# A transformer layer on one core: the end by sequence, feed-forward halves between small products, and three transfers moved

## The chip, the core and the metric

The kernel runs on one core of a Trainium2 chip. TensorE (PE in the profile) multiplies, VectorE (DVE), ScalarE (ACT) and GpSimd (POOL) work on elements, SyncE (SP) issues most transfers. The metric is the device time of one execution in microseconds. The kernel before took 1822.03 us in the median of three runs (1814.67 to 1822.35).

## The reference

The program is one decoder layer on x of 32 sequences, 256 positions, 256 features, in float32:

```python
x = x + attn(layernorm(x))            # causal self-attention, 16 heads of 16, 4 key heads, low-rank q (64) and kv (32), rotary
x = x + xattn(layernorm(x), ctx)      # cross-attention on ctx, 16 heads, masked by an int mask of 256 x 256
x = x + ffn(layernorm(x))             # relu(x @ w1.T + b1) rounded to 8 bits, times w2 rounded to 8 bits, plus b2
```

Softmax is exact: the maximum of each row of scores is subtracted before the exponential. Query and key are each cut into three bf16 parts, stacked to 96 rows (`TERMS = 6` pairs of 16), so that one bf16 product gives a float32 score.

## The kernel before

Two sequences form a group; there are 16 groups. The order of every engine is written by hand, each engine in its own block, tied by semaphores. Three parts make a program: a prologue, `body(i, prev, nxt)` for each group (groups 1 to 14 in a hardware loop), and an end. `prev` means that a group before still has its cross-attention and feed-forward to do, `nxt` that a next group is prepared.

A body on PE goes through these stages:

1. **Cross exponentials** of the group before (`attend(st, 1, i - 1, "scores")`): 16 tiles of transposed scores (`cross_shifted`, L1279), ACT's exponential (L691), DVE's bound for three tiles of four (L922), and the products with the values three tiles later (`times_v`, L1318). The stacked queries carry three more rows, the negated row maxima (`negT`), which come by a transfer (`put_neg`, L372). PE waits for those of the first sequence at tile 0, for the second at tile 8.
2. **Self maxima** (`self_scores`, L1202 and L1213): 12 tiles, each reduced by DVE (L900). PE also does `v2`, `k2_1` and the output product of the group before (L1404).
3. **Self exponentials** (`attend(st, 0, i, None)`, L1256 and L1261): 12 tiles; PE waits for the negated maxima of the second sequence at its seventh tile.
4. **The middle chain**: output product, two normalisations, `query2` (L1165) for each sequence, the small products of the next group, `query1` (`q0`, `q1`, L1173, 64 rows), `key1` (`k`, L1179, 32 rows) and `value1` (`v_0`, `v_1`, L1189, 32 rows), and feed-forward tiles 0 to 2 of the group before (`hidden`, L1149). It takes turns through four PSUM banks (`body_users` says which name stands in which).
5. **Cross maxima** (`cross_scores`, L1237): 16 tiles; ACT lays the mask down (`premask`, L737), DVE reduces (L900), PE does feed-forward tiles 3 to 7 (L1435) and the second feed-forward product (L1451) between them. POOL meanwhile rotates, cuts and rounds the next group's q and k (L509 to L537).

SP issues the transfers that stack the parts: `put_part` (`Q<-q1p`, `K<-k1p`, `K<-k2p`), `put_query2` (`Q<-q2p`), `put_neg`, and `swap_pairs` for the rotation. It waits for each in the order written, so one that isn't ready holds those behind it. POOL ends a body with `add_ffn` (L498), which adds the feed-forward to `x3`, and stores it (L500). DVE waits for the store before last in the next body (`y_stored`) ahead of `residual(st, "out2", 0, ...)`.

In the prologue SP loads x, then 15 weights in one list counted by one semaphore (`loaded`). DVE rotates q, rounds `w2` and only then cuts q; POOL rotates and cuts k (L509 to L537); SP stacks all parts of both (L354, L356); PE waits for all of them before its first score (L1202). The end does both sequences' output product, one normalisation over four blocks, eight feed-forward tiles of 512 columns (L1149), and two output products (L1451).

## Time and profile before

| | us |
|---|---|
| median of three runs | 1822.03 |
| profiled execution | 1819.02 |
| its span, first to last instruction | 1817.0 |
| PE busy | 1673.7 |
| DVE busy | 1245.2 |
| ACT busy | 1103.6 |
| POOL busy | 724.2 |

The span runs from the first instruction to the last; the profiled execution's own time is 2.0 us longer. A busy PE is one that has a matmul under way. The page also shows the clock that PE was granted, as a share of 2.4 GHz. What decides is which wait ends last in a stage, so the stages are read one by one in the rows further down.

### The profile page before, as it was taken

What the parts mean: (1) busy time and instruction counts of PE and PEld (TensorE: products, weight loads), DVE (VectorE), ACT (ScalarE), POOL (GpSimd) and SP (SyncE); (2) the same over time, 40 slices, a digit from 0 to 9 for tenths busy, and PEclk for the clock granted to TensorE, in tenths of its full rate; (3) what the DMA queues carried; (4) which work ended last, traced back from release to release, by engine and by line L of the source; (5) the groups of instructions that cost most, each with busy time, mean ns of one, the idle gap of its engine ahead of it and who ended that gap; (6) DMA issues with size and microseconds to landing.
All of it is one profiled execution on the core that took longest, in us unless ns stands there. A gap on an engine that the chain in (4) does not pass through costs nothing.

```text
span 1817.0 us, 34264 instructions
## 1 busy us (share of the span) xinstructions
PE 1673.7 (92%) x12274; PEld 1015.8 (56%) x12274; DVE 1245.2 (69%) x1908; ACT 1103.6 (61%) x1704; POOL 724.2 (40%) x962
## 2 busy tenths in 40 slices
PE   3779999999999999999999999999999999999987
PEld 1445556556555565555556555665655556555554
DVE  4567486785848768586776848678585876858582
ACT  3355675756667565665756567575666756566572
POOL 3251353624435352433634345362443535243310
PEclk9979999999999999999999999999999999999998
DMA  6452552715346251633724255271534625163320
GB/s 170 59 83 39 76 88 36 122 28 85 57 64 100 36 95 38 92 67 43 121 36 79 49 75 88 36 119 30 84 59 62 101 36 95 37 93 57 48 37 12
DMA packets 86606, 124.07 MB, mean 68 GB/s; under 512 B 10481, under 2 KB 53938, under 8 KB 86322
## 3 DMA queue, kind: packets, MB, share of 16 engines
q1 hardware_dynamic: 83650, 115.26, 41.5%
q0 software_dynamic: 2160, 7.87, 1.2%
q10 hardware_dynamic: 768, 0.57, 0.1%
q8 instruction: 18, 0.29, 0.1%
q14 instruction: 10, 0.08, 0.0%
HBM read 21.42 MB, written 8.39 MB: 16 GB/s over the span
## 4 chain that ended last, share of the span: by engine, by line
PE 68%; DVE 10%; issue 7%; ACT 5%; POOL 4%; DMA 3%; SPq 2%; ACTq 0%; POOLq 0%
PE o_pair L1318 12%; PE small L1404 8%; PE small L1149 7%; DVE negmax L900 6%; PE score L1279 6%; PE o_pair L1149 3%; PE small L1331 3%; PE small L1165 3%; PE score L1256 3%; DMA Q<-negT 2%; PE small L1435 2%; PE score L1202 2%; DVE P L922 2%; PE score L1261 2%; ACT P L691 2%
## 5 line engine op out<-in xcount | busy, mean ns | idle before, releaser
L691 ACT ACTIVATE P<-score 128x1024 f32<-128x1024 f32 x448 | 446.8, 1026 | 119.7 <-PE score L1279 42.7
L900 DVE TENSOR_REDUCE negmax<-score 128x4 f32<-128x1024 f32 (+1 forms) x384 | 460.0, 1219 | 32.6 <-PE score L1237 19.8
L922 DVE TENSOR_TENSOR P<-P,cross_bound 128x1024 f32<-128x1024 f32 x192 | 255.6, 1365 | 65.8 <-ACT P L691 65.6
L1318 PE MATMUL o_pair<-P,V 128*32 128x256 f32 (+1 forms) x4096 | 283.1, 363 | 15.6 <-DVE P L922 15.6
L737 ACT ACTIVATE score<-cross_q 128x1024 f32<-128x1024 bf16 x192 | 196.5, 1023 | 60.3 <-DVE negmax L900 58.7
L468 POOL TENSOR_TENSOR negrest<-negmax,negparts 128x32 f32<-128x32 f32 x64 | 15.5, 243 | 502.1 <-ACT negparts L652 501.6
L1318 PEld LDWEIGHTS o_pair<-P,V 128*32 128x32 f32 x4096 | 86.2, 108 | 148.2 <-issue 78.1
L1279 PE MATMUL score<-Q,K 99*128 99x256 bf16 x1024 | 151.5, 275 | 13.3 <-DMA Q<-negT 12.2
L1435 PE MATMUL small<-xnT,w 128*128 128x256 f32 x600 | 156.7, 379 | 0.0
L1237 PE MATMUL score<-K,Q 96*128 96x256 bf16 x768 | 119.5, 279 | 33.8 <-ACT score L737 30.8
L1279 PEld LDWEIGHTS score<-Q,K 99*128 99x128 bf16 x1024 | 85.8, 98 | 100.8 <-issue 66.1
L547 POOL TENSOR_SCALAR_AFFINE_SELECT P<-P 128x512 f32<-128x512 f32 (+1 forms) x160 | 121.1, 757 | 0.0
L461 POOL TENSOR_TENSOR rstd<-vareps,minus_half 128x2 f32<-128x2 f32 x32 | 22.4, 701 | 236.2 <-DVE vareps L881 236.2
L910 DVE RECIPROCAL rsum<-small 128x16 f32<-128x16 f32 x127 | 32.2, 253 | 118.7 <-PE small L1331 118.7
L966 DVE SCALAR_TENSOR_TENSOR q2f<-small,bq,q2p 128x256 f32<-128x256 f32 x64 | 28.0, 479 | 124.3 <-ACT q2p L722 124.3
L1237 PEld LDWEIGHTS score<-K,Q 96*128 96x128 bf16 x768 | 70.6, 99 | 73.3 <-ACT score L737 53.0
L1435 PEld LDWEIGHTS small<-xnT,w 128*128 128x128 f32 x600 | 102.8, 189 | 13.4
L684 ACT ACTIVATE o_sb<-o_pair 128x512 f32<-128x512 f32 x128 | 75.9, 593 | 52.3 <-PE o_pair L1318 52.3
L652 ACT ACTIVATE negparts<-negmax 128x32 bf16<-128x32 f32 x64 | 14.4, 225 | 130.4 <-DVE negmax L900 130.4
L1202 PE MATMUL score<-K,Q 96*128 96x256 bf16 x512 | 78.7, 276 | 6.4 <-DMA Q<-q1p 6.4
L900 DVE TENSOR_REDUCE negmax<-o_pair 128x4 f32<-128x1024 f32 x64 | 78.1, 1221 | 8.2 <-PE o_pair L1242 8.2
L1331 PE MATMUL small<-ident,o_sb 128*128 128x128 f32 x508 | 81.6, 283 | 0.2 <-ACT o_sb L684 0.2
(181 smaller groups left out, 3219.4 us busy)
## 6 DMA issues: line engine op xcount, KB each, us to landing
Q<-q1p SPq DMA_DIRECT2D x96, 256.0 KB, 5.9
K<-k2p SPq DMA_DIRECT2D x96, 256.0 KB, 8.4
Q<-q2p SPq DMA_DIRECT2D x192, 128.0 KB, 4.0
x_in<-in_x SPq DMA_DIRECT2D x16, 512.0 KB, 5.6
ctxT<-in_ctx SPq DMA_DIRECT2D x16, 512.0 KB, 4.4
k2f<-q1f SPq DMA_DIRECT2D x32, 256.0 KB, 5.3
out_y<-x POOLq DMA_DIRECT2D x15, 512.0 KB, 3.6
K<-k1p SPq DMA_DIRECT2D x96, 64.0 KB, 4.5
```

The lines of the kernel that those rows point to most:

```text
L547: G.affine_select(out=p, in_=p, compare_op=ALU.is_ge, fill=0.0, base=0, pattern=[[0, heads], [1, 128]], channel_multiplier=-1).then_inc(pr ...
L691: A.activation(P[:, t % 4, :], score[b][:, :, :], ACT.Exp, scale=SCALE).then_inc(score_free[b], 1)
L737: A.activation(cross_bufs[n][:, :, :].rearrange("p c (j k) -> p (c j) k", j=2), cross_q[:, t // 4 % 2, :].unsqueeze(1).broadcast_to([128, ...
L900: V.tensor_reduce(negmax[:, k, h:h + 1024 // w], s.rearrange("p (h w) -> p h w", w=w), AX.X, ALU.max, negate=True).then_inc(score_free[b], 1)
L922: V.tensor_tensor(p, p, cross_bound[:, t % 2, :].unsqueeze(1).broadcast_to([128, 4, SEQ]), ALU.min).then_inc(probs_masked[1], 1)
L1149: last = T.matmul(bank[0:rows, :], w[:, c, cols], src[:, c, :], start=c == 0, stop=c == NC - 1)
L1237: last = T.matmul(cross_bufs[n][:, c, SEQ * j:SEQ * j + SEQ], Q2[0:KROWS, b, h, 128 * (k % 2):128 * (k % 2) + 128], K2[0:KROWS, h, SEQ * b ...
L1279: last = T.matmul(score[n][:, c, SEQ * j:SEQ * j + SEQ], K2[:, h, SEQ * b + 128 * kb:SEQ * b + 128 * kb + 128], Q2[:, b, h, :], start=j == ...
L1318: last = T.matmul(o_ps[ob][32 * j:32 * j + 32, SEQ * gg + q0:SEQ * gg + SEQ], v, p, start=s == 0, stop=end, tile_position=(0, 32 * j), ski ...
L1331: last = T.transpose(bank[:, 256 * k + 128 * gg:256 * k + 128 * gg + 128], o_sb[:, u % 2, SEQ * gg + 128 * k:SEQ * gg + 128 * k + 128], id ...
L1404: last = T.matmul(bank[:, DM * k:DM * k + DM], src[:, c, at:at + 128], w[:, c, :], start=c == 0, stop=c == NC - 1)
L1435: last = T.matmul(bank[:, half], w1[:, c, 128 * t:128 * t + 128], xnT3[:, c, half], start=p == 0, stop=c == NC - 1, skip_group_check=True)
```

## The change

- **Middle chain.** PE's order becomes `q0`, first half (128 input features) of feed-forward tile 1, `q1`, its second half, `k`, tile 2 in two halves, `xnT2_1`, `v_0`, `v_1`, `query2` of the second sequence. ACT's copies follow the same order, and the banks are dealt anew.
- **Feed-forward addition.** POOL waits, where a next group is prepared, until DVE has reduced tile 0 of the next self maxima, and then does `add_ffn`.
- **Order of transfers.** In a body five of the six `K<-k2p` transfers are issued before the second sequence's `negT` for self-attention. The first sequence's `negT` for cross-attention is issued before `K<-k1p`.
- **Prologue.** mask, b2 and w2 are loaded first with semaphores of their own, and DVE does its mask and rounding work before the rotation. DVE rotates and cuts q of the first sequence, k, and then q of the second. The q parts are stacked by sequence in transfers of 128 KB, the k parts from POOL's queue, and PE begins with what the first sequence needs. ACT's rows of ones are written in pieces.
- **End.** Output product, normalisation, feed-forward and the second product go one sequence after the other, in tiles of 256 columns.

The core of the diff:

```diff
-              + n("qa") + ["xnT2_0", "out1_1", "q2_0"] + n("q0", "q1") + n("k", "v_0", "v_1")
-              + p("h1") + ["xnT2_1"] + p("h2") + ["q2_1"])
+              + n("qa") + ["xnT2_0", "out1_1", "q2_0"] + n("q0") + p("h1") + n("q1", "k") + p("h2")
+              + ["xnT2_1"] + n("v_0", "v_1") + ["q2_1"])
...
+            sp.dma_start(mask[:, :, :], d["mask"]).then_inc(loaded_mask, 16)
+            sp.dma_start(b2[:, :], d["b2"]).then_inc(loaded_w2, 16)
+            sp.dma_start(w2[:, :, :], d["w2"]).then_inc(loaded_w2, 16)
...
-                put_part("k1", n, 0)
-                put_part("q1", n, 0)
+                sp.wait_ge(first_q1, (4, 6, 7)[n])
+                put_queries(n, 0, stacked_first)
+            for n in range(3):
+                sp.wait_ge((part1, part2, part3)[n]["q1"], 1)
+                put_queries(n, 1, stacked["q1"])
...
-                for b in range(GB):
-                    put_neg(st, 0, b)
-                for n in range(3):
+                put_neg(st, 0, 0)
+                for n in range(2):
                     put_part("k2", n, i)
+                put_neg(st, 0, 1)
+                put_part("k2", 2, i)
...
                     put_part("q1", 0, i + 1)
+                put_neg(st, 1, 0)
+                if nxt:
                     put_part("k1", 0, i + 1)
-                put_neg(st, 1, 0)
-                if nxt:
...
-            rope_products("k1", cosk, sink, k1s, 0)
-            rope_sum("k1", k1s, 0)
-            rest("k1", 0)
-            third("k1", 0)
+            for n in range(3):
+                pool.wait_ge((part1, part2, part3)[n]["k1"], 1)
+                for t, p in enumerate(K_PART):
+                    if p == n:
+                        pool.dma_start(K1[HD * t:HD * t + HD], k1p[:, n, :]).then_inc(stacked_first_k1, 16)
...
                 if prev:
+                    if nxt:
+                        n, before = tile("S1", i + 1, 0)
+                        pool.wait_ge(score_free[n], before + 1)
                     add_ffn(st, i - 1)
...
                 if nxt:
                     turn(st, "q1", q1f[:, 1, :])
+                premask(i, 0)
+                if prev:
+                    hidden(st, [1])
+                if nxt:
                     turn(st, "k", k1f[:, :], rows=KV_HEADS * HD)
+                if prev:
+                    hidden(st, [2])
+                turn_batch(st, "xnT2_1", 1, inT)
+                if nxt:
                     values1(st)
-                premask(i, 0)
-                if prev:
-                    hidden(st, [1])
-                turn_batch(st, "xnT2_1", 1, inT)
                 premask(i, 1)
-                if prev:
-                    hidden(st, [2])
                 query2_first(st, i, 1)
                 query2_second(st, 1)
...
+            for b in range(GB):
+                at = range(2 * b, 2 * b + 2)
+                residual(END, "out2", b, x3, x2)
+                residual_done(END, "out2", b)
+                norm_stats(2, x3, NG - 1 + b, at, at)
+                if b == 0:
+                    normalise(END, 1, 3, NG - 1)
+                norm_apply(2, x3, NG - 1 + b, at)
...
-                    for c in range(NC):
-                        query1(st, c)
+                    query1(st, 0)
+                if prev:
+                    hidden_half(st, 1, 0)
+                if nxt:
+                    query1(st, 1)
+                if prev:
+                    hidden_half(st, 1, 1)
+                if nxt:
                     key1(st)
+                if prev:
+                    hidden_half(st, 2, 0)
+                    hidden_half(st, 2, 1)
...
+            batch_copied(END, "oT2_0")
+            tokens(END, "out2", inT, wo2, 0)
+            unit_turn(END, 1, NG - 1, 3)
+            for u in range(2, UNITS):
+                pe.wait_ge(small_free[END.bank(f"o2t{u}")], END.this(f"o2t{u}"))
+            turned_batch(END, "oT2_1", 1, o)
+            pe.wait_ge(xn_ready[2], NG)
+            turned_batch(END, "xnT3_0", 0, xn)
+            batch_copied(END, "oT2_1")
             tokens(END, "out2", inT, wo2, 1)
-            pe.wait_ge(xn_ready[2], NG)
-            for c in range(NC):
-                turned(END, f"xnT3_{c}", xn, c)
-            copied(END, "xnT3_")
-            hidden(END, range(HT))
-            pe.wait_ge(small_free[END.bank(f"h{HT - 1}")], END.this(f"h{HT - 1}"))
-            for r in range(2):
-                ffn_out(END, r)
+            batch_copied(END, "xnT3_0")
+            end_hidden(0)
+            pe.wait_ge(xn_ready[2], NG + 1)
+            turned_batch(END, "xnT3_1", 1, xn)
+            ffn_ready(0)
+            ffn_out(END, 0)
+            batch_copied(END, "xnT3_1")
+            end_hidden(1)
+            ffn_ready(1)
+            ffn_out(END, 1)
```

PE in the loop's middle chain, from `query2` of the first sequence (L1165) to that of the second; `xnT,w` is a feed-forward product, `ident,xn` a transposition. Before:

```order
L1165 MATMUL small<-inT,wq 128x256 x4
L1173 MATMUL small<-qaT,wqb 128x512
L1173 MATMUL o_pair<-qaT,wqb 128x512
L1179 MATMUL o_pair<-qaT,wk 64x512
L1184 REGISTER_ALU
L1189 MATMUL small<-wv,qaT 128x64 x4
L1147 REGISTER_ALU
L1149 MATMUL o_pair<-xnT,w 128x512 x2
L1342 MATMUL o_pair<-ident,xn 128x128 x4
L1147 REGISTER_ALU
L1149 MATMUL small<-xnT,w 128x512 x2
L1358 REGISTER_ALU
L1165 MATMUL small<-inT,wq 128x256 x4
```

After (`query2` is L1239):

```order
L1239 MATMUL small<-inT,wq 128x256 x4
L1247 MATMUL small<-qaT,wqb 128x512
L1223 MATMUL o_pair<-xnT,w 128x512
L1247 MATMUL o_pair<-qaT,wqb 128x512
L1223 MATMUL o_pair<-xnT,w 128x512
L1251 REGISTER_ALU
L1253 MATMUL small<-qaT,wk 64x512
L1223 MATMUL small<-xnT,w 128x512 x2
L1412 REGISTER_ALU
L1416 MATMUL o_pair<-ident,xn 128x128 x4
L1263 MATMUL o_pair<-wv,qaT 128x64 x2
L1258 REGISTER_ALU
L1263 MATMUL small<-wv,qaT 128x64 x2
L1432 REGISTER_ALU
L1239 MATMUL small<-inT,wq 128x256 x4
```

Each feed-forward product of 512 columns now has a small one before or behind it, and the value products stand alone behind the transposition.

SP in the loop from the load of `ctxT` to the loop's end, before:

```order
L412 DMA ctxT<-in_ctx 128x1024
L348 REGISTER_ALU
L356 DMA Q<-q1p 16x8x1024 x3
L354 DMA K<-k1p 16x4x512 x3
L370 REGISTER_ALU
L372 DMA Q<-negT 3x16x256
L356 DMA Q<-q1p 16x8x1024 x2
L354 DMA K<-k1p 16x4x512 x2
L356 DMA Q<-q1p 16x8x1024
L354 DMA K<-k1p 16x4x512
```

After:

```order
L430 DMA ctxT<-in_ctx 128x1024
L351 REGISTER_ALU
L359 DMA Q<-q1p 16x8x1024 x3
L381 REGISTER_ALU
L383 DMA Q<-negT 3x16x256
L357 DMA K<-k1p 16x4x512 x3
L359 DMA Q<-q1p 16x8x1024 x2
L357 DMA K<-k1p 16x4x512 x2
L359 DMA Q<-q1p 16x8x1024
L357 DMA K<-k1p 16x4x512
```

`Q<-negT` went ahead of the three `K<-k1p`.

SP at the loop's self maxima and exponentials, before:

```order
L372 DMA Q<-negT 3x16x256
L370 REGISTER_ALU
L372 DMA Q<-negT 3x16x256
L370 REGISTER_ALU
L372 DMA Q<-negT 3x16x256
L348 REGISTER_ALU
L356 DMA K<-k2p 16x8x1024 x6
```

After:

```order
L383 DMA Q<-negT 3x16x256
L381 REGISTER_ALU
L383 DMA Q<-negT 3x16x256
L351 REGISTER_ALU
L359 DMA K<-k2p 16x8x1024 x5
L381 REGISTER_ALU
L383 DMA Q<-negT 3x16x256
L359 DMA K<-k2p 16x8x1024
```

The third `Q<-negT` is the second sequence's; five transfers of the key stack now stand ahead of it.

## Rows read from the trace of the kernel before

**Rows 1.** Stages; columns: stretch, its us, busy us (instructions) per engine, granted clock, DMA, GB/s.

```profile
868.90:893.90 25.00, 22.09 (x145) 16.26 (x143) 21.30 (x19) 18.62 (x31) 20.80 (x20) 1.00 0.71 113
893.90:915.20 21.30, 20.37 (x191) 9.84 (x191) 17.65 (x20) 16.90 (x21) 6.25 (x5) 1.00 0.48 83
120.40:144.30 23.90, 17.55 (x64) 8.46 (x65) 18.20 (x16) 13.87 (x18) 18.70 (x21) 0.50 0.80 109
1786.00:1796.40 10.40, 7.12 (x14) 3.76 (x15) 1.38 (x4) 1.97 (x4) 1.03 (x1) 0.51 0.00 0
```

**Rows 2.** The same view: ten us from `q0` on, first and last of eight.

```profile
426.70:436.70 10.00, 10.00 (x30) 4.83 (x29) 2.90 (x8) 7.02 (x15) 3.56 (x5) 0.83 0.81 131
...
1614.00:1624.00 10.00, 10.00 (x29) 5.00 (x29) 2.95 (x8) 7.09 (x15) 3.56 (x5) 0.83 0.80 131
```

**Rows 3.** Timeline of PE, middle of two groups; columns: start, us, instruction, [idle before <-releaser].

```profile
430.60 3.45 PE L1149 MATMUL o_pair<-xnT,w 128*128 128x512 f32 x4
...
859.29 1.12 PE L1173 MATMUL small<-qaT,wqb 64*128 64x512 f32 x2
...
863.23 1.98 PE L1149 MATMUL o_pair<-xnT,w 128*128 128x512 f32 x4
...
867.21 1.89 PE L1165 MATMUL small<-inT,wq 128*128 128x256 f32 x8
```

**Rows 4.** Waits of PE over the span: us in total, times, longest.

```profile
PE o_pair L1318 <- DVE P L922: 15.6, 17, 1.3
...
PE score L1279 <- DMA Q<-negT: 12.2, 15, 3.1
```

**Rows 5.** Chain of waits, end of a group; columns: start, us, what.

```profile
890.53 3.24 DMA Q<-negT
...
893.91 1.04 PE score L1279 x8
...
898.35 2.85 DVE P L922
```

**Rows 6.** Timeline of PE, the same place in a group after a half-clock stretch.

```profile
463.10 1.04 PE L1279 MATMUL score<-Q,K 99*128 99x256 bf16 x8 [0.46 <-DMA Q<-negT]
```

**Rows 7.** Timeline, DVE and POOL side by side, and POOL's next wait.

```profile
875.71 2.34 DVE L900 TENSOR_REDUCE negmax<-score 128x4 f32<-128x1024 f32 x2
...
875.81 2.35 POOL L515 TENSOR_TENSOR q1f<-q1f,k2f 128x1024 f32<-128x1024 f32 x1
...
896.99 3.12 POOL L498 TENSOR_TENSOR x<-x,ffn 128x1024 f32<-128x1024 f32 x1
...
925.59 0.24 POOL L468 TENSOR_TENSOR negrest<-negmax,negparts 128x32 f32<-128x32 f32 x1 [23.95 <-ACT negparts L652]
```

**Rows 8.** Timeline of SP's queue: maxima rows and the key stack.

```profile
929.40 10.66 SPq L372 DMA_DIRECT2D Q<-negT  x2
940.18 3.86 SPq L356 DMA_DIRECT2D K<-k2p  x6
```

**Rows 9.** Transfers `K<-k2p` of one group: issue to landing.

```profile
DMA to landing us min/median/max: 4.4/8.3/11.8
```

**Rows 10.** Timeline of PE: seventh tile of the self exponentials.

```profile
943.19 0.60 PE L1256 MATMUL score<-Q,K 99*128 99x512 bf16 x2
```

**Rows 11.** Chain of waits before the first scores.

```profile
24.38 2.23 DMA k1s<-k1f
...
40.84 11.09 DMA Q<-q1p
```

**Rows 12.** Timeline: a DVE subtraction of 128 x 512 elements.

```profile
861.85 0.69 DVE L972 TENSOR_TENSOR q2p<-q2f,q2p 128x512 bf16<-128x512 f32 x1 [0.70 <-ACT q2p L730]
```

**Rows 13.** Twelve transfers `Q<-q2p`, 128 KB each: issue to landing.

```profile
DMA to landing us min/median/max: 3.2/4.2/4.9
```

**Rows 14.** Chain of waits at the end.

```profile
1791.25 16.50 PE small L1149 x32
...
1813.05 0.60 ACT ffn L759
```

More of the change, by code:

```diff
@@ L1014, in _, with product, summed @@
             V.tensor_copy(cross_q[:, :, :], maskf[:, :, :]).then_inc(mask_step, 1)
+            dve.wait_ge(loaded_w2, 32)
+            V.tensor_copy(w2q[:, :, :], w2[:, :, :], saturate=False)
+            V.tensor_copy(b2q[:, :], b2[0:1, :])
+            def product(t, table, done, of=None):
+                V.tensor_tensor(t, t, table[:, :] if len(t.shape) == 2 else
+                                table[:, :].unsqueeze(1).broadcast_to([table.shape[0], t.shape[1], SEQ]),
+                                ALU.mult).then_inc(done, 1)
+            def summed(t, other, done):
+                V.tensor_tensor(t, t, other, ALU.add).then_inc(done, 1)
+            dve.wait_ge(loaded_self, 16 * LOADS_SELF)
+            dve.wait_ge(swapped["q1"], 32)
+            q, other = [[t[:, :, SEQ * b:SEQ * b + SEQ] for b in range(GB)] for t in (q1f, q1s)]
+            k, other_k = [t[:, :].rearrange("p (b q) -> p b q", q=SEQ) for t in (k1f, k1s)]
+            product(q[0], cosq, first_q1)
+            product(other[0], sinq, first_q1)
+            dve.wait_ge(swapped["k1"], 32)
+            product(k, cosk, cosine["k1"])
+            product(other_k, sink, sine["k1"])
+            dve.wait_ge(first_q1, 2)
+            summed(q[0], other[0], first_q1)
+            dve.wait_ge(cosine["k1"], 1)
+            dve.wait_ge(sine["k1"], 1)
+            summed(k, other_k, whole["k1"])
+            product(q[1], cosq, cosine["q1"])
+            dve.wait_ge(first_q1, 4)
+            V.tensor_tensor(q[0], q[0], q1p[:, 0, :, 0:SEQ], ALU.subtract).then_inc(first_q1, 1)
+            dve.wait_ge(part1["k1"], 1)
+            V.tensor_tensor(k1f[:, :], k1f[:, :], k1p[:, 0, :], ALU.subtract).then_inc(rest1["k1"], 1)
+            product(other[1], sinq, sine["q1"])
+            dve.wait_ge(first_q1, 6)
+            V.tensor_tensor(q1p[:, 2, :, 0:SEQ], q[0], q1p[:, 1, :, 0:SEQ], ALU.subtract).then_inc(first_q1, 1)
+            dve.wait_ge(part2["k1"], 1)
+            V.tensor_tensor(k1p[:, 2, :], k1f[:, :], k1p[:, 1, :], ALU.subtract).then_inc(part3["k1"], 1)
+            dve.wait_ge(cosine["q1"], 1)
+            dve.wait_ge(sine["q1"], 1)
+            summed(q[1], other[1], whole["q1"])
             bk = PRO.bank("maskT")
@@ L1384, in attend @@
                         times_v(st, a, g, t - LAG)
+                    if at_end == "last" and t == n:
+                        for u in range(2):
+                            pe.wait_ge(small_free[st.bank(f"o2t{u}")], st.this(f"o2t{u}"))
+                        turned_batch(st, "oT2_0", 0, o)
                     u = (t - LAG - 2) // TPU[a] - 1
@@ L1601, in _ @@
-            pe.wait_ge(small_free[END.bank("oT2_1")], END.this("oT2_1"))
-            tokens(END, "out2", inT, wo2, 1)
-            pe.wait_ge(xn_ready[2], NG)
-            for c in range(NC):
-                turned(END, f"xnT3_{c}", xn, c)
-            copied(END, "xnT3_")
-            hidden(END, range(HT))
-            pe.wait_ge(small_free[END.bank(f"h{HT - 1}")], END.this(f"h{HT - 1}"))
-            for r in range(2):
-                ffn_out(END, r)
+            attend(END, 1, NG - 1, "last")
@@ new lines, in end_hidden @@
+            def end_hidden(b):
+                at = slice(SEQ * b, SEQ * b + SEQ)
+                for j in range(HT // 2):
+                    bk = END.bank(f"h{b}_{j}")
+                    pe.wait_ge(small_free[bk], END.before(f"h{b}_{j}"))
+                    bank, filled = small[bk], small_full[bk]
+                    for n in range(2):
+                        t = 2 * j + n
+                        for c in range(NC):
+                            last = T.matmul(bank[:, SEQ * n:SEQ * n + SEQ], w1[:, c, 128 * t:128 * t + 128],
+                                            xnT3[:, c, at], start=n == 0 and c == 0, stop=c == NC - 1,
+                                            skip_group_check=True)
+                    last.then_inc(filled, 1)
```

156 lines of the change are left out of this document (79 added, 77 removed).

## The prediction

> **What bounds the kernel now.** I read the busy time by stage first, then PE's waits, then the chain of waits at the places with the longest ones, and last the timeline around each. In the cross exponentials of a steady group PE is busy for 20.37 of 21.30 us, in the cross maxima for 22.09 of 25.00 [rows 1]. So PE sets the time, and what counts is where it idles and where its clock falls. Four places stand out.
>
> First, the clock. In eight of the fourteen loop groups the ten microseconds from `q0` on show a mean granted clock of 0.83, in the other six 1.00 [rows 2], which holds the first and the last of the eight. PE is busy for all 10.00 us in both kinds. The low piece sits on feed-forward tile 1, which follows the four small products: 3.45 us at 430.60, against 1.98 at 863.23 [rows 3]. That is 1.2 GHz in place of 2.4.
>
> Second and third, two waits. PE waited 12.2 us in 15 waits for the `negT` transfer and 15.6 us in 17 for DVE's bound [rows 4].
>
> Fourth, the two ends. The first score starts at 51.93, when the last of twelve stacking transfers lands [rows 11]. The last group's end runs one stage behind the other and at half clock for its first part: 0.51 over 10.40 us, with PE busy for 7.12 [rows 1].
>
> **The change part by part.** The sum is made against the profiled execution, 1819.0 us, of which the span is 1817.0. It lies 3 us under the median of the runs shown. How many groups meet the low clock may differ between executions, and a forecast that removes the low stretches lands at the same time from either.
>
> *The clock in the middle chain.* At 0.83 over 10 us, 0.17 x 10 = 1.7 us of full-speed work is lost in a stretch where PE never stops. Eight groups make 13.6 us. PE keeps the same products. Before, it did `q0`, `q1`, `k`, `v_0`, `v_1` in a row, 3.94 us of products on 64 or 32 rows of the array (859.29 to 863.23 [rows 3]). Now no more than one of them stands between products on 128 rows, except for the values, about 1 us. I take the whole 13.6; the bounds are 0 and 13.6. The Trainium skill (TensorE: Matmul & The Clock Gate, HAM oscillation) ties the fall to PE's idle gaps or waits. By it these stretches, which follow no gap, would not come from the small products, and mixing wouldn't cure them; that is a rival below. This trace doesn't agree so far: PE is busy for 10.00 of 10.00 us there [rows 2].
>
> *The waits inside the middle chain.* From `q0` to the second `query2` it is 7.92 us (859.29 to 867.21 [rows 3]). In the new order ACT must finish tile 2's copy before it copies `xnT2_1`, while PE has only the values to do. I see PE reach `query2` between 0.3 us earlier and 0.3 later, and take 0. Over 15 groups the bounds are -4.5 and +4.5.
>
> *`negT` before `K<-k1p`.* The chain shows the transfer issued at 890.53, landed 3.24 us later, and PE starting at 893.91 [rows 5]. Three `K<-k1p` were issued in front of it, about 0.6 us each, and they waited for POOL's part of k. Now it goes 2.2 us earlier. It still queues behind three `Q<-q1p` and should land about 892.2, before PE's arrival at 892.95 (893.91 less its wait). The wait of 0.94 goes. In a group that met the low clock it was 0.46 [rows 6], because POOL's chain doesn't feel PE's clock: without the low stretch it would be 0.94 there too. So 14 x 0.94 = 13.2 us, of which 4 would only appear once the clock is mended. The first group waits 3.1 [rows 4]; there POOL and ACT are late next, and I take 1.2 of it. What is late next in the others is ACT's first exponentials, held by POOL's cut of the other maxima. That costs some tenths that the following tiles, still in PE's shadow, take back. Bounds: 8 and 16 for all.
>
> *The feed-forward addition.* DVE's bound at 898.35 took 2.85 us [rows 5] beside POOL's addition, which ran 3.12 us from 896.99 [rows 7]. Freed of it I expect about 1.2, and PE's wait behind it, 0.92 in each of 14 groups, goes: 12.9 us of the 15.6 [rows 4]. (The other three waits are the last group's, whose addition isn't moved.) Beside the self maxima POOL meets `TENSOR_REDUCE`, and that one isn't slowed: two took 2.34 us beside a POOL sum of two tensors [rows 7]. POOL's next work came at 925.59, after 23.95 us of idleness [rows 7], and the addition ends about 921. The store issued behind it, whose landing DVE needs only about 934, has ten microseconds. Queued behind POOL's new wait is only the cut of the next self maxima, wanted later. Bounds: 7 and 14.
>
> *Key stack before the second `negT`.* This one costs. Six `K<-k2p` issued from 940.18 landed from 4.4 to 11.8 us after their issues [rows 8, 9], so the last at 943.4 + 11.8 = 955.2 and one each 2.1 us. Issued from 930.2, right behind the first `negT` (929.40 [rows 8]), the fifth lands about 943.1. The second `negT` is issued at 939.35 and stands behind it. PE wants it at 943.19 [rows 10]. I expect it at 943.2 to 943.7, a wait of 0.3, and PE has nothing else to do: 16 x 0.3 = 4.8 us. Bounds: 0, and 1.0 in each, 16. Nothing is gained, for the stack is wanted some 14 us after it lands.
>
> *The prologue.* k's swapped halves land at 26.6 (24.38 + 2.23 [rows 11]). From there twelve DVE steps of about 0.65 (a 128 x 512 subtraction takes 0.69 [rows 12]) give the last part of the first sequence's q and of k at about 34.2; before, POOL and DVE passed turns until 40.84 [rows 11]. The rounding work that stood in DVE's way moves into its idle time before. Six q transfers of half the size follow one each microsecond: twelve like them landed 3.2 to 4.9 us after issue [rows 13]. POOL's six k transfers share the engines, and its last is issued about 36. First score: 40, against 51.97, so 12 us. Bounds: 44 (if the shorter rows move at half the rate) and 38.5, that is 8 and 13.5. The second sequence's q is wanted ten microseconds later and lands by 47.
>
> *The end.* Before, ACT copied the last product at 1813.05 [rows 14]. Now the first sequence's output product starts about 1.3 us earlier, its normalisation and transposition are done at 1783.8, and its feed-forward starts at 1785.7, against 1791.25 [rows 14]. The 32 products of 512 columns took 16.50 us [rows 14]; at full clock they are 32 x 0.43 = 13.8. Chain: 6.9 for the first half, 0.6 transposition, 0.5 for ACT, 2.2 output product, 6.9, 1.0 for ACT's last copy, 2.1, so the last copy stands at 1806. That is 7 us. An idle stretch of about 2 us before it may still cost the clock once, so I take 6.5; bounds 3 and 8.
>
> Sum: -13.6 (clock) -13.2 -1.2 (`negT`) -12.9 (addition) +4.8 (key stack) -12.0 (prologue) -6.5 (end) = -54.6, and 1819.0 - 54.6 = 1764.4. I predict 1764.
>
> **The rivals.**
> *The clock is not mended.* For it: PE is busy for all ten microseconds in either kind of group [rows 2], so how much it works is not what differs from other stages; the values still stand alone. Against: the low stretch comes only behind the four products. Time: 1764 + 13.6 = 1778. The rule of the Trainium skill named above gives this one.
> *The key stack holds PE.* For it: the landing computed above is at the very time of the need. If it is 1 us late in each group, 16 - 4.8 = 11 more: 1775.
> *The gains are handed back.* PE arrives 1.9 us earlier at tiles where ACT (16.90 busy of 21.30) or POOL (20.80 of 25.00) is late next [rows 1]. If half of the 26 us of waits comes back under other names: 1777.
> *Slower.* In the first group the clock stayed at 0.50 for 23.9 us once it had fallen [rows 1], in cross maxima without feed-forward work between them. If the values, alone behind a transposition and followed by ACT's copy, let it fall and it stays low through the cross maxima in the loop, a group loses up to half of PE's 22.09 us, 11 us. The point from which it decides is the 55 us gained over 15 groups, 3.7 us each: low for more than 7.4 us in each group is slower than before. At the full 11 us: 1764 + 165 = 1929. Against it: fourteen groups recovered at once.
>
> **How the numbers follow.** The forecast has 0.66, the unmended clock 0.13, the key stack 0.09, gains handed back 0.09, the slower case 0.02; 0.01 is left for changes that don't bite at all. The forecast's own range is 1756 to 1772. Stretched to the three milder rivals it is 1753 to 1780, with low ends from the prologue, the end and a key stack that costs nothing. What a measurement of this kernel tells from no change is about 0.5%, 9 us; all cases but the last two lie beyond it. Faster 0.96, same 0.02, slower 0.02.
>
> **What would show it.** The granted clock at 1.00 in all loop groups and a group period without two values; no wait on `negT` at the first cross exponential, perhaps one at the seventh self exponential; DVE's bounds at 1.2 us all; the first score near 40; the last ACT copy about seven microseconds nearer to the loop's end. Wrong would be a stretch at half clock behind the value products, or PE waiting on ACT for as long as it waited on the transfer.

## The result, and the profile after

The changed kernel takes 1792.05 us (1790.97 to 1792.66, four runs) against 1822.19 before: ratio 0.9842, 95% interval [0.9815, 0.9869]. That is 30 us less. I had forecast 1764, with a range of 1753 to 1780. The sign was right, and half of the gain is missing.

The profiled execution spans 1791.0 us. This is its busy time by stage, for the ten microseconds from `q0` in one group and for that group's cross maxima and cross exponentials (columns as in [rows 1]):

```profile
953.57:963.57 10.00, 10.00 (x34) 4.76 (x34) 2.94 (x8) 7.39 (x15) 3.56 (x5) 1.00 0.81 130
963.97:987.07 23.10, 21.92 (x146) 16.36 (x144) 19.97 (x19) 17.85 (x29) 19.77 (x17) 1.00 0.66 107
987.07:1008.90 21.83, 20.65 (x193) 9.67 (x191) 16.73 (x21) 17.65 (x23) 3.48 (x6) 1.00 0.45 66
```

The granted clock is 1.00 in all fourteen loop groups, where eight had shown 0.83 [rows 2]. The cross maxima are 1.9 us shorter than in [rows 1]. But the cross exponentials are 0.5 longer, although PE's waits for DVE's bound [rows 4] have left that stage. PE's waits over the span name what stands there now, in place of the two of [rows 4]:

```profile
PE score L1353 <- ACT P L716: 16.2, 15, 1.2
PE score L1311 <- ACT score L764: 15.5, 32, 3.0
PE score L1276 <- DMA K<-k1p: 14.8, 1, 14.8
PE score L1330 <- DMA Q<-negT: 12.6, 15, 0.9
```

L1353 is the cross exponentials' score, L1330 that of the self exponentials, L716 ACT's exponential. Fifteen waits of 1.1 in the mean and fifteen of 0.84 are new. (The waits for DVE's bound that are left, 2.4 us in two, are the last group's.) A group lasts, from its first self score to that of the next:

```profile
901.79 0.61 PE L1276 MATMUL score<-K,Q 96*128 96x256 bf16 x4
...
1008.88 0.61 PE L1276 MATMUL score<-K,Q 96*128 96x256 bf16 x4
```

This is 107.1 us. Before it was 106.8 in a group that kept its clock (808.39 to 915.20) and 108.6 in one that didn't. By my terms it should have become 106.8 - 0.94 - 0.92 + 0.3 = 105.2. The 1.9 that are missing, times the fourteen loop groups, are 27 us of an error of 28. The two ends came out within 1.3 us of the forecast. So the question is what the loop's group lost.

The first new wait, in the timeline of all engines at the start of the cross exponentials:

```profile
988.00 1.02 ACT L716 ACTIVATE P<-score 128x1024 f32<-128x1024 f32 x1
...
989.06 1.23 DVE L978 TENSOR_TENSOR P<-P,cross_bound 128x1024 f32<-128x1024 f32 x1 [1.44 <-ACT P L716]
989.08 1.30 POOL L486 TENSOR_TENSOR negrest<-negmax,negparts 128x32 f32<-128x32 f32 x1
...
990.42 0.23 ACT L683 ACTIVATE negparts<-negrest 128x32 bf16<-128x32 f32 x1 [1.39 <-POOL negrest L486]
990.55 1.01 ACT L716 ACTIVATE P<-score 128x1024 f32<-128x1024 f32 x1
...
991.62 0.61 PE L1353 MATMUL score<-Q,K 99*128 99x256 bf16 x4 [1.17 <-ACT P L716]
```

POOL's cut of the maxima (the step that splits the negated maxima into bf16 parts) takes 1.30 us; elsewhere it took 0.24 [rows 7]. It starts 0.02 us after DVE's bound and ends 0.09 after it. ACT has its second rounding (L683) queued in front of exponential 1, waits 1.39 for the cut, and PE waits 1.17 for the score buffer.

The same collision stood at the same place in the kernel before, on the next step of the cut:

```profile
894.80 0.24 POOL L468 TENSOR_TENSOR negrest<-negmax,negparts 128x32 f32<-128x32 f32 x1
895.70 2.41 DVE L922 TENSOR_TENSOR P<-P,cross_bound 128x1024 f32<-128x1024 f32 x2 [2.36 <-ACT P L691]
895.86 1.17 POOL L475 TENSOR_TENSOR negparts<-negrest,negparts 128x32 bf16<-128x32 f32 x1 [0.82 <-ACT negparts L658]
```

There the third part met DVE's bound, took 1.17 in place of 0.25 and held nobody whose wait shows, while the cut before it, for which ACT's exponential 1 waits, was through. The earlier start moved the collision one step forward.

The second new wait, in the timelines of SP's queue and of PE (compare [rows 8, 10]):

```profile
916.00 0.74 SPq L383 DMA_DIRECT2D Q<-negT  x1
916.87 3.22 SPq L359 DMA_DIRECT2D K<-k2p  x5
925.95 0.75 SPq L383 DMA_DIRECT2D Q<-negT  x1
928.70 0.57 SPq L359 DMA_DIRECT2D K<-k2p  x1
...
930.68 0.60 PE L1330 MATMUL score<-Q,K 99*128 99x512 bf16 x2 [0.82 <-DMA Q<-negT]
```

The transfer is 24 KB and needs 4.7 us from issue to use, behind five of 256 KB.

At the ends: the first score (before: 51.97) and ACT's last copy.

```profile
41.24 1.01 PE L1276 MATMUL score<-K,Q 96*128 96x256 bf16 x4 [14.85 <-DMA K<-k1p]
...
1732.86 1.22 PE L1353 MATMUL score<-Q,K 99*128 99x256 bf16 x8
...
1787.02 0.60 ACT L786 ACTIVATE ffn<-small 128x512 f16<-128x512 f32 x1 [2.36 <-PE small L1532]
```

From the last group's first cross exponential to the end of the span it is now 58.1 us (1732.86 to 1791.0), before 65.0 (1752.03 to 1817.0). The span, 26.0 us shorter in all, divides so: 10.7 less up to the first score, 1.0 more in the first group, 10.0 less in the fourteen loop groups, 0.6 more from there to the last group's first cross exponential, and 6.9 less behind it. In the loop the eight half-clock stretches took 14.4 with them, and the groups without one became 0.3 longer.

### The profile page after: what moved, and what is told of

Its sections match the earlier page's. It is cut to its first block, busy times and chain, and to the rows that moved or that the text cites. A ratio compares the mean times of both kernels' runs of the same rounds, so it can differ in the third digit from the quotient of the medians.

```text
span 1791.0 us, 34372 instructions
## 1 busy us (share of the span) xinstructions
PE 1673.0 (93%) x12306; PEld 1012.3 (57%) x12306; DVE 1209.0 (68%) x1920; ACT 1102.5 (62%) x1715; POOL 709.2 (40%) x964
## 4 chain that ended last, share of the span: by engine, by line
PE 67%; DVE 9%; POOL 8%; ACT 5%; DMA 5%; issue 5%; ACTq 0%; SPq 0%; DVEq 0%; POOLq 0%
PE o_pair L1392 12%; PE small L1482 8%; DVE negmax L956 6%; PE score L1353 6%; PE small L1223 5%; DMA Q<-negT 4%; PE small L1405 4%; PE small L1239 3%; PE o_pair L1223 3%; PE score L1330 3%; PE small L1516 2%; PE score L1276 2%; POOL q1p L555 2%; POOL q1f L540 2%; PE score L1359 1%
## 5 line engine op out<-in xcount | busy, mean ns | idle before, releaser
L716 ACT ACTIVATE P<-score 128x1024 f32<-128x1024 f32 x448 | 446.9, 1027 | 109.2 <-PE score L1330 50.7
L956 DVE TENSOR_REDUCE negmax<-score 128x4 f32<-128x1024 f32 (+1 forms) x384 | 460.1, 1219 | 29.7 <-PE score L1311 20.4
L978 DVE TENSOR_TENSOR P<-P,cross_bound 128x1024 f32<-128x1024 f32 x192 | 234.0, 1248 | 78.6 <-ACT P L716 78.4
L1353 PE MATMUL score<-Q,K 99*128 99x256 bf16 x1024 | 156.4, 275 | 17.2 <-ACT P L716 16.2
L516 POOL TENSOR_TENSOR x<-x,ffn 128x1024 f32<-128x1024 f32 x15 | 33.0, 2197 | 294.3 <-DVE negmax L956 294.3
L1353 PEld LDWEIGHTS score<-Q,K 99*128 99x128 bf16 x1024 | 84.4, 98 | 108.4 <-ACT P L716 56.2
L486 POOL TENSOR_TENSOR negrest<-negmax,negparts 128x32 f32<-128x32 f32 x64 | 30.4, 474 | 192.3 <-ACT negparts L677 191.0
L1330 PE MATMUL score<-Q,K 99*128 99x512 bf16 x256 | 74.9, 383 | 16.3 <-DMA Q<-negT 12.6
```

Source lines behind the costliest of these rows:

```text
L716: A.activation(P[:, t % 4, :], score[b][:, :, :], ACT.Exp, scale=SCALE).then_inc(score_free[b], 1)
L956: V.tensor_reduce(negmax[:, k, h:h + 1024 // w], s.rearrange("p (h w) -> p h w", w=w), AX.X, ALU.max, negate=True).then_inc(score_free[b], 1)
L978: V.tensor_tensor(p, p, cross_bound[:, t % 2, :].unsqueeze(1).broadcast_to([128, 4, SEQ]), ALU.min).then_inc(probs_masked[1], 1)
L1330: last = T.matmul(score[n][:, c, :], K1[:, kh, SEQ * b:SEQ * b + 128], Q1[:, 4 * kh + 2 * c:4 * kh + 2 * c + 2, SEQ * b:SEQ * b + SEQ], st ...
L1353: last = T.matmul(score[n][:, c, SEQ * j:SEQ * j + SEQ], K2[:, h, SEQ * b + 128 * kb:SEQ * b + 128 * kb + 128], Q2[:, b, h, :], start=j == ...
```

## The experiments

All times are medians; each kernel ran beside the kernel before, whose median was 1816.8 to 1822.3 in these comparisons. In the texts on record "theory" is what I held after reading the trace above.

| kernel | built on | us | lowest to highest | ratio to before, interval |
|---|---|---|---|---|
| second_neg_first | after | 1779.12 | 1777.95 to 1780.63 | 0.9766 [0.9743, 0.9789] |
| cross_neg_back | after | 1791.59 | 1790.53 to 1793.82 | 0.9841 [0.9818, 0.9864] |
| middle_back | after | 1815.40 | 1811.87 to 1818.97 | 0.9966 [0.9953, 0.9979] |
| add_back | after | 1803.68 | 1802.20 to 1804.46 | 0.9904 [0.9882, 0.9927] |
| act_cut_later | second_neg_first | 1771.37 | 1770.14 to 1772.02 | 0.9731 [0.9693, 0.9770] |
| cut_later_neg_back | act_cut_later | 1776.54 | 1775.16 to 1778.58 | 0.9766 [0.9726, 0.9805] |
| whole_tile | act_cut_later | 1771.56 | 1771.23 to 1771.81 | 0.9734 [0.9695, 0.9773] |
| pool_cut_first | second_neg_first | 1771.56 | 1768.09 to 1772.48 | 0.9736 [0.9697, 0.9775] |
| x_after_neg | pool_cut_first | 1761.96 | 1758.19 to 1762.55 | 0.9670 [0.9649, 0.9690] |
| three_small | x_after_neg | 1760.73 | 1760.15 to 1762.38 | 0.9668 [0.9646, 0.9691] |
| both_cuts | x_after_neg | 1761.25 | 1758.30 to 1763.26 | 0.9669 [0.9644, 0.9693] |
| before_mixed | before | 1805.06 | 1801.29 to 1808.68 | 0.9912 [0.9893, 0.9930] |

### The key stack's price: second_neg_first

```diff
-                put_neg(st, 0, 0)
-                for n in range(2):
-                    put_part("k2", n, i)
-                put_neg(st, 0, 1)
-                put_part("k2", 2, i)
+                for b in range(GB):
+                    put_neg(st, 0, b)
+                for n in range(3):
+                    put_part("k2", n, i)
```

> The changed kernel with the second negT of the self maxima issued before all K<-k2p again; all else as changed. My theory: the wait 'PE score <- DMA Q<-negT' of 0.82 to 0.84 us at the seventh self exponential goes in 15 groups and nothing else becomes late behind it, 12.6 us off 1792: 1779 to 1781. Rival (the gain is handed back): PE only waits longer for ACT's exponentials or for o, and the time stays within 4 us of 1792. K<-k2p is still wanted long after it lands, so nothing is lost by either.

Measured 1779.1: 12.9 us less. PE's longest waits have no `negT` among them any more:

```profile
PE score L1275 <- DMA K<-k1p: 16.3, 1, 16.3
PE score L1352 <- ACT P L715: 16.2, 15, 1.2
PE score L1310 <- ACT score L763: 14.3, 32, 2.5
```

The key stack issued early costs 12.9 us and gains nothing. Nothing became late behind the mended wait: a loop group lasts 106.2 us in place of 107.1.

### The first cross `negT`: cross_neg_back

```diff
-                put_neg(st, 1, 0)
                 if nxt:
                     put_part("k1", 0, i + 1)
+                put_neg(st, 1, 0)
+                if nxt:
                     for n in range(1, 3):
```

> The changed kernel with the first cross negT issued behind K<-k1p part 0 again; all else as changed. The forecast's own view: the wait of 0.94 us at the first cross exponential comes back in 14 groups and the first group loses 1.2 more: 1792 + 13 to 14 = 1806. My theory now: the earlier start only brought DVE's bound on the first tile (989.06) onto POOL's cut of the maxima (989.08, 1.30 us in place of 0.24), ACT waits 1.39 for it and PE 1.17. With the transfer back in its old place the cut is done before DVE's bound starts, takes 0.24 again, and the 1.17 go while the 0.94 come: 1789 to 1795.

Measured 1791.6, no difference (0.5 us). My forecast gave this edit 14.4. The timeline of this kernel at the same place shows the exchange, PE's wait against POOL's:

```profile
987.43 1.05 PE L1354 MATMUL score<-Q,K 99*128 99x256 bf16 x8 [0.93 <-DMA Q<-negT]
...
988.34 0.24 POOL L487 TENSOR_TENSOR negrest<-negmax,negparts 128x32 f32<-128x32 f32 x1
...
989.08 0.22 ACT L684 ACTIVATE negparts<-negrest 128x32 bf16<-128x32 f32 x1
989.20 1.02 ACT L717 ACTIVATE P<-score 128x1024 f32<-128x1024 f32 x1
989.21 2.41 DVE L979 TENSOR_TENSOR P<-P,cross_bound 128x1024 f32<-128x1024 f32 x2 [2.32 <-ACT P L717]
```

PE waits 0.93. Counted from the group's first self score (901.09 here, 901.79 in the changed kernel), POOL's cut starts at the same time, 87.25 against 87.29, and DVE's bound 0.85 later, 88.12 against 87.27. So the cut is through 0.6 us ahead of the bound, in 0.24. The third part behind it takes 1.17 beside the bound, as in the kernel before, and no engine's wait for it shows. A loop group is even 0.4 shorter than in the changed kernel (106.7 against 107.1), 5.6 us over the loop. The first group is 1.4 longer, near the 1.2 that I had given it; but that group lasts 107.5 to 113.1 us in the traces with the new prologue, so single traces don't show this. The end is 1.7 longer (59.8 against 58.1) in the profiled execution, which fell to half clock once there. The medians' 0.5 adds up all of these.

### The middle chain: middle_back and before_mixed

```diff
-              + n("qa") + ["xnT2_0", "out1_1", "q2_0"] + n("q0") + p("h1") + n("q1", "k") + p("h2")
-              + ["xnT2_1"] + n("v_0", "v_1") + ["q2_1"])
+              + n("qa") + ["xnT2_0", "out1_1", "q2_0"] + n("q0", "q1") + n("k", "v_0", "v_1")
+              + p("h1") + ["xnT2_1"] + p("h2") + ["q2_1"])
```

middle_back has this and the old order of the same work on ACT and PE; before_mixed is the reverse edit on the kernel before.

> The changed kernel with the middle chain of the kernel before (q0, q1, k, v_0, v_1, then tiles 1 and 2), in the bank table, ACT and PE; all else as changed. Two terms of opposite sign: from q0 to the second query2 7.9 us in place of 8.6, 15 x 0.67 = 10 us less; and the granted clock falls again behind the value products in some of the 14 loop groups, 1.7 us each. My theory: 1782 if no group falls, 1796 if eight do; by the forecast's view (mixing costs nothing): 1792 to 1806. Rival: what cured the clock was something else (the groups' period), then no group falls and 1782.

> The kernel before with nothing changed but the middle chain (bank table, ACT, PE). Forecast's view: the clock's term, 13.6 us for eight groups and 0 for the chain: about 1808 against 1822. Added up from the other experiments: 1792 with the second negT first (-12.9), the addition back (+11.6), the cross negT back (-0.5), the old prologue (+10.8) and end (+6.9) gives 1808: 1805 to 1811, clock 1.00 in all loop groups. Rival (the middle chain gains 23 us wherever it is put, as middle_back showed on the changed kernel): 1799.

middle_back: 1815.4, 23.3 us more, and outside what either view allowed. The half clock came back in ten of the fourteen loop groups, in one of them twice (the second time within the cross maxima). This is read from the slowest of its ten executions, 1819.0. Two of its groups, ten microseconds from `q0`:

```profile
747.20:757.20 10.00, 10.00 (x29) 4.90 (x29) 2.99 (x9) 6.96 (x15) 3.56 (x5) 0.83 0.80 130
966.30:976.30 10.00, 10.00 (x39) 5.58 (x39) 2.92 (x8) 7.72 (x16) 3.56 (x5) 1.00 0.81 130
```

A group with it lasts 109.5 us, one without 107.1 to 107.2, just as long as with the mixed chain. So what mended the clock was not the groups' length, and a fall costs 2.3 here. Of these, 1.65 are PE's from `q0` to the second `query2` (9.56 us against 7.91), and 0.62 come behind it, at the fifth tile of the cross maxima. ACT lays the mask down for that tile behind its copies of the middle chain, and PE waits 1.80 for it where it otherwise waits 1.18:

```profile
766.01 0.61 PE L1310 MATMUL score<-K,Q 96*128 96x256 bf16 x4 [1.80 <-ACT score L764]
```

In the kernel before the same two parts stand (1.68 and 0.62, in the groups from 1023.81 and 808.39), and a fall cost 1.8 only, for behind it PE waited 0.47 for `negT` in place of 0.96 [rows 6]; here that cover is gone. And the 0.67 us by which the mixed chain is longer cost nothing. PE's timeline of the chain in the changed kernel shows those 0.67:

```profile
953.57 1.12 PE L1247 MATMUL small<-qaT,wqb 64*128 64x512 f32 x2
954.62 1.12 PE L1223 MATMUL o_pair<-xnT,w 128*128 128x512 f32 x2
955.68 1.12 PE L1247 MATMUL o_pair<-qaT,wqb 64*128 64x512 f32 x2
956.73 1.13 PE L1223 MATMUL o_pair<-xnT,w 128*128 128x512 f32 x2
957.78 1.07 PE L1253 MATMUL small<-qaT,wk 32*64 32x512 f32 x2
...
962.16 1.99 PE L1239 MATMUL small<-inT,wq 128*128 128x256 f32 x8
```

From `q0` to the second `query2` it is 8.59, against 7.92 [rows 3]: a pair of products takes 1.05, where in the old order one took 0.91 to 1.0. The changes between products on different numbers of rows account for nearly all of it: whole_tile below, with two changes fewer, takes 8.40, and three_small, with `q0`, `q1` and k in a row, 8.01. PE gets it back at the fifth tile of the cross maxima, where it waits for ACT's mask copy, in middle_back (first row) and in the changed kernel (second):

```profile
982.77 0.61 PE L1310 MATMUL score<-K,Q 96*128 96x256 bf16 x4 [1.18 <-ACT score L764]
```

```profile
970.05 0.61 PE L1311 MATMUL score<-K,Q 96*128 96x256 bf16 x4 [0.38 <-ACT score L764]
```

before_mixed: 1805.1, 15.2 less than the kernel before in the same comparison (1820.3), with a loop group of 106.8 us throughout, as the groups without a fall had before. My forecast said 13.6; the fourteen loop groups together are 14.7 shorter. The rival of 23 falls. In middle_back's trace the loop is 24.8 longer: nine groups with one stretch at 2.3 each and one with two at 4.0. In the kernel before it is eight at 1.8.

### The addition: add_back

```diff
                 if prev:
-                    if nxt:
-                        n, before = tile("S1", i + 1, 0)
-                        pool.wait_ge(score_free[n], before + 1)
                     add_ffn(st, i - 1)
```

> The changed kernel with POOL's feed-forward addition unwaited, behind the cut of the maxima again; all else as changed. Forecast's view: DVE's bound takes 2.8 us beside it, PE waits 0.92 longer in 14 groups: 1792 + 13 = 1805. Rival (that gain was handed back too, since ACT's exponentials end the stretch anyway): 1792 to 1796.

Measured 1803.7, 11.6 us more. PE's wait for the bound is in sixteen places again, two of them the last group's, now 7.4 us in all; the wait for ACT that comes first may take a part of it. A loop group lasts 107.8 us in place of 107.1:

```profile
PE score L1350 <- ACT P L713: 16.2, 15, 1.2
...
PE o_pair L1389 <- DVE P L975: 7.4, 16, 1.3
```

Moving the addition is worth what I gave it (12.9), within 1.3 us.

### The cut: act_cut_later, pool_cut_first, cut_later_neg_back

act_cut_later, in ACT's exponentials:

```diff
-                    if t == 0 and a == 1:
+                    if t == 1 and a == 1:
                         cut_second(a, g, 1)
```

pool_cut_first, on POOL:

```diff
                     part("k1", 1, rest1, part2, i + 1)
-                    third("k1", i + 1)
                 cut_rest(1, i, 1)
+                if nxt:
+                    third("k1", i + 1)
                 cut_third(1, i, 1)
```

> Second negT first (as in second_neg_first, 1779.1) and in the cross exponentials ACT's second rounding of the maxima behind exponential 1 in place of exponential 0. My theory: PE's 1.17 us at the fourth score tile is ACT's wait for POOL's cut, which DVE's bound slows to 1.30. Behind exponential 1 that wait shrinks to about 0.35, exponential 2 starts at +3.3 us of the stage in place of +4.0, 0.69 x 15 = 10 us less: 1767 to 1771. Rival (ACT's exponentials bound the stretch as a whole and would be late somewhere else): 1776 to 1780.

> Second negT first, and on POOL the cut of the second sequence's maxima ahead of k's third part (1.15 us) in place of behind it; ACT unchanged. My theory: the cut runs before DVE's bound begins and takes 0.24 us again, ACT waits for nothing, exponential 1 starts 1.3 earlier: 1.04 to 1.17 x 15 = 16 to 18 us under 1779.1: 1762 to 1764. If the cut stays at 1.3 us although it starts before the bound (rival: its 1.30 has another cause than DVE): gain of less than 10, above 1769.

> act_cut_later with the first cross negT behind K<-k1p part 0 again. My theory: the 0.94 us that the changed order takes off PE's wait are real but were covered by ACT's wait for the cut; with that one mended, undoing the order costs: 7 to 10 us above act_cut_later. Rival: the order of that transfer is worth nothing in any case, within 2 us of act_cut_later.

act_cut_later: 1771.4, 7.7 less, where I expected 8 to 12. The cut still takes 1.31 beside the bound there, but ACT waits only 0.48 for it in place of 1.39. pool_cut_first: 1771.6, 7.6 less, where I expected 16 to 18. The mechanism held there, and half of the gain did not come. POOL's timeline, and then PE:

```profile
973.35 0.25 POOL L485 TENSOR_TENSOR negrest<-negmax,negparts 128x32 f32<-128x32 f32 x1 [0.25 <-ACT negparts L677]
973.55 1.15 POOL L554 TENSOR_TENSOR k1p<-k1f,k1p 64x512 bf16<-64x512 f32 x1
974.67 1.22 POOL L492 TENSOR_TENSOR negparts<-negrest,negparts 128x32 bf16<-128x32 f32 x1
...
976.40 0.41 SPq L415 DMA_DIRECT2D x_in<-in_x  x1
978.05 0.81 SPq L383 DMA_DIRECT2D Q<-negT  x1
...
982.72 0.61 PE L1353 MATMUL score<-Q,K 99*128 99x256 bf16 x4 [0.62 <-DMA Q<-negT]
```

The cut takes 0.25 ahead of DVE's bound. The third part (L492), which took 0.25 in the changed kernel, meets the bound and takes 1.22. The 1.17 of PE is gone, but eight tiles on PE arrives early at the second `negT`, which isn't there yet: 0.62.

cut_later_neg_back: 1776.5, 5.2 more than act_cut_later. With the cut out of the way the order of the cross `negT` is worth 5 us; I had expected 7 to 10. Together with cross_neg_back (0.5) it shows the gain as real and covered by the wait for the cut.

### What held the second `negT`: x_after_neg, both_cuts

```diff
-                if nxt:
-                    sp.wait_ge(xn_ready[0], i + 1)
-                    sp.wait_ge(x1b_ready, i + 1)
-                    sp.dma_start(x_in[:, :, :], x_v[i + 1]).then_inc(x_loaded, 16)
                 if prev:
                     put_neg(st, 1, 1)
+                if nxt:
+                    sp.wait_ge(xn_ready[0], i + 1)
+                    sp.wait_ge(x1b_ready, i + 1)
+                    sp.dma_start(x_in[:, :, :], x_v[i + 1]).then_inc(x_loaded, 16)
```

> pool_cut_first with the next group's x_in (256 rows of 1 KB for each of two sequences) issued behind the second cross negT in place of ahead of it. In pool_cut_first that negT was issued at 978.05, 1.65 us behind x_in, and PE waited 0.62 for it at 982.72, 14 times 10.3 us in all. My theory: it queued behind x_in's transfers and lands 1 to 2 us earlier without them; 14 x 0.65 = 9 us off 1771.6: 1762 to 1764. x_in is wanted only at 988.5, so nothing else waits. Rival (the stretch is ACT's: 16 exponentials and their like end it whatever PE waits for): 1769 to 1772.

> x_after_neg with ACT's second rounding behind exponential 1 as well (both cures of the cut). With the cut done in time ACT waits for nothing either way; exponential 1 starts 0.2 earlier: 0 to 3 us less than x_after_neg. If the second negT is wanted before it lands again, since its rounding now comes 1 us later: 3 to 8 more.

x_after_neg: 1762.0, 9.6 less, as expected. No wait for `negT` is left among PE's longest, and the load of 512 KB itself lands 3.6 us after its issue where it took 5.6. A group now lasts 104.8:

```profile
886.90 0.61 PE L1276 MATMUL score<-K,Q 96*128 96x256 bf16 x4
...
991.72 0.61 PE L1276 MATMUL score<-K,Q 96*128 96x256 bf16 x4
```

both_cuts: 1761.3, no further gain. x_after_neg is 57 us under the kernel before of its comparison and 30 under the changed kernel. It is the version to take.

### How much mixing the clock needs: whole_tile, three_small

whole_tile does feed-forward tile 1 in one piece behind `q0`, and `q1` and k stand in a row. three_small puts `q0`, `q1` and k in a row, then both tiles, and only the values behind the transposition; the banks and ACT's copies follow.

```diff
 # three_small, PE
-                    query1(st, 0)
-                if prev:
-                    hidden_half(st, 1, 0)
-                if nxt:
-                    query1(st, 1)
-                if prev:
-                    hidden_half(st, 1, 1)
-                if nxt:
+                    for c in range(NC):
+                        query1(st, c)
                     key1(st)
                 if prev:
-                    hidden_half(st, 2, 0)
-                    hidden_half(st, 2, 1)
+                    hidden(st, [1])
+                    hidden(st, [2])
```

> act_cut_later with feed-forward tile 1 undivided in the middle chain: q0, tile 1, q1, k, tile 2, transposition, values. Two changes of shape fewer. My theory: the chain is some 0.2 us shorter, and that is given back at ACT's mask copies, as the undivided chain's 0.67 were: within 2 us of act_cut_later, clock 1.00 in all groups. Rivals: the 0.2 count (3 us less); or q1 and k in a row let the clock fall in some groups, 2.3 us each (up to 30 more).

> x_after_neg with q0, q1 and k in a row again, then tiles 1 and 2, the transposition and the values: only the values are moved away from the other small products. If the clock falls only behind all five in a row, as in the kernel before: within 2 us of x_after_neg and 1.00 in all groups. If three in a row (2.9 us) are enough in some groups: 2.3 us for each, up to 30 more. I hold the first for likelier (0.6).

Both took the time of the kernel they were built on (1771.6 against 1771.4, 1760.7 against 1762.0), with no half clock behind the small products in any loop group. One of three_small:

```profile
623.10:633.10 10.00, 10.00 (x37) 5.44 (x37) 2.94 (x8) 7.46 (x15) 3.57 (x5) 1.00 0.80 131
```

So the alternation in halves, which is the visible part of this edit, isn't needed: taking the two values away from `q0`, `q1` and k was enough in these traces.

## Why the prediction was right or wrong

**The clock: right, its size in part by luck.** 13.6 us forecast, 15.2 measured by before_mixed, and 1.00 in all loop groups. The stretches came from the small products in a row, while PE stood busy for all of the time [rows 2]; in the ten microseconds ahead of `q0` it was busy for 10.00 of 10.00 as well, in groups with and without a fall. I took 1.7 for each fall, the time at half clock. It was 1.7 in the chain, plus 0.62 at ACT's mask copy, which I didn't have, less 0.49 at `negT`. That last part I had read [rows 6], and still counted both the 1.7 and the full 0.94 for `negT`, which counts 3.8 us twice over eight groups (in before_mixed PE waits 16.0 us for `negT` at this place, against 12.2 [rows 4]). The two slips roughly cancel. The rule of the Trainium skill (TensorE: Matmul & The Clock Gate, HAM oscillation), which asks for idle gaps, does not describe these falls; taking the products apart cured them with no gap removed.

**The middle chain: right in the sum, wrong in its reason.** I gave 0. The chain is 0.67 longer, outside my 0.3, by the changes between products on different numbers of rows. It costs nothing because the cross maxima wait for ACT's mask copies anyway.

**`negT` before `K<-k1p`: the step that failed.** I forecast -13.2 in the loop and -1.2 in the first group. cross_neg_back measured nothing in all. The transfer did land in time and the 0.94 did go. What failed is the sentence on what is late next: "ACT's first exponentials, held by POOL's cut of the other maxima. That costs some tenths that the following tiles, still in PE's shadow, take back." The engine and the instruction were right. The size was not: the cut became 1.30 in place of 0.24, because the earlier start put DVE's bound on top of it, and nothing took the resulting 1.17 back. In a loop group I forecast 0.94 gained, and 0.4 was lost; the first group may have gained. Over the execution it is 14.4 forecast against nothing measured, half of the error of 28. It is also the sign that I had named for being wrong: PE waiting on ACT for as long as it waited on the transfer. The row that should have warned me stood in my own list: DVE's bound at 2.85 beside POOL's addition [rows 5, 7]. I used that conflict for the addition and did not ask for which other POOL instruction it holds. A plainer one stood in the same microseconds of the trace before: the third part of this very cut, 1.17 at 895.86 in place of 0.25. The Trainium skill (SBUF — State Buffer, Who interferes with whom) states it in general for the ports that DVE and GpSimd share: a DVE instruction with two inputs in SBUF and a GpSimd instruction that reads SBUF exclude each other, and the one that starts second waits for the other's end. This trace agrees: 989.06 + 1.23 = 990.29, and the cut that started at 989.08 ended at 990.38.

**The key stack: the right mechanism, mis-sized.** +4.8 forecast, 12.9 measured. The wait was at the place named, 0.82 to 0.84 in place of 0.3. The transfer landed 4.7 us after its issue; I had left it some 3.9 to 4.3. Fifteen groups times 0.5 are the 8 us. Its upper bound of 16 held it.

**The feed-forward addition: right.** 12.9 forecast, 11.6 measured. DVE's bounds in the loop are back at 1.2 us. Beside the self maxima it takes 2.13 us in place of 3.12 [rows 7], and DVE's reductions keep their mean of 1219 ns.

**The prologue and the end: right in the sum, read from the traces alone.** First score at 41.24 (forecast 40), 10.7 gained of 12.0; in the eleven variants with this prologue it stands at 39.6 to 41.7. The time came out by two errors that cancel: I had the last `K<-k1p` leave about 36 and land some 4 us later, and it left at 34.03 and took 7.07. The end is 6.9 us shorter, forecast 6.5. That execution kept its clock there, and so did one other; in ten variants the end takes 59.2 to 59.8, with one stretch at half clock, which is 5.2 to 5.8 gained and which I had allowed for. Neither part was undone by an experiment.

**The sum.** -15.2 (clock) + 0.5 (`negT`) - 11.6 (addition) + 12.9 (key stack) - 10.7 - 6.9 (the ends) = -31.0. From 1819.0 (the profiled execution) or 1822.2 (the median) that leads to 1788 or 1791, against 1792. The one to four us that are left I can't split; the terms were measured on different bases and overlap, as the addition's wait and ACT's do in add_back.

**The rivals.** "Gains handed back" (1777, 0.09) was the one that happened, stronger than I priced it: I let half of 26 us come back, and what came back was the whole of one term. "The key stack holds PE" (1775) happened too, 8 of the 11 us. Each alone was in the range; both together, 14.4 + 8, were not (1787), and I had added up no pair of them. With the two waits mended and `x_in` moved, the time is 1762: the forecast's terms exist, and the kernel as changed doesn't collect them.

## What to carry to other kernels

When a wait is taken away, lay the following five microseconds of every engine over each other at the new time, not only the chain that waits: here an engine that came 0.94 us earlier met another's short instruction and lost 1.17. Where a trace shows two engines slowing each other in one pair of instructions, look for every other pair of the same kind that the change brings together. A small transfer that PE waits for goes in front of large ones that nobody waits for yet, and this holds for loads as for stacks; count the large ones that are still under way at its issue. When two rivals rest on different places in the loop, give their sum a place in the range.

## What the runs showed of the hardware

- TensorE's clock fell from 2.4 to 1.2 GHz with PE busy for 10.00 of 10.00 us (0.83 as the mean), behind `q0`, `q1`, k and the values in a row, 3.94 us of products on 64 or 32 rows: in eight of fourteen loop groups of the kernel before and ten of fourteen in middle_back. With the values moved behind a transposition it fell in no loop group of any trace, three_small's included.
- POOL's subtraction of 128 x 32 elements took 0.24 us alone, and 1.30 beside a DVE minimum of two SBUF tensors (1.17 and 1.22 at two other starts); next to DVE's reduction of a score it took 0.25 (912.77 in the changed kernel).
- Neighbouring PE products of 512 columns that change between 64 and 128 rows took 1.05 us a pair, against 0.91 to 1.0 in the old order.
- A transfer of 24 KB took 4.7 us from issue to use behind five of 256 KB, and another landed 3.24 us after its issue behind three of 64 KB [rows 5].
